# Local masks written into the score banks by ScalarE, for the next group, in place of TensorE's two identity products

## What is computed

```python
def local_attention(q, k, v):          # w = 32, 8 windows a sequence
    bk2, bv2 = (look(bk), look(bv))    # keys of the window before and of its own: 64
    mask = (it < jb) | (it > jb + w) | (jb == -1)
    sim = jnp.einsum('bhwie,bhwje->bhwij', bq, bk2) * QK_SCALE
    sim = jnp.where(mask, -jnp.finfo(sim.dtype).max, sim)
    attn = jax.nn.softmax(sim, -1)
    return jnp.einsum('bhwij,bhwje->bhwie', attn, bv2)

for i in range(DEPTH):                 # 6
    x = attn_layer(shift_tokens(x), Wqkv[i], q_scale[i], k_scale[i], Wo[i]) + x
    x = ffn_layer(shift_tokens(x), ln_g[i], ln_b[i], W1[i], b1[i], W2[i], b2[i]) + x
```

## Time and profile before

| | |
|---|---|
| median of 3 runs | 1949.55 us (1947.46 to 1950.31) |
| the profiled execution, its own time | 1953.01 us |
| its span | 1951.2 us |
| TensorE busy | 1860.3 us, 95% |
| VectorE busy | 1581.5 us, 81% |
| ScalarE busy | 1405.6 us, 72% |
| GpSimd busy | 1372.8 us, 70% |
| mask products L940 | 384, busy 73.6 us |
| granted TensorE clock, mean | 0.997 |

### The profile page before, as it was taken

The page is one execution under the profiler, slowest core; times in us unless marked ns, Lnnn a source line. Parts: engine busy times, 40 slices in busy tenths (PEclk is TensorE's granted clock), DMA queues, the critical chain, the costliest instruction groups (busy, mean ns, idle before and its releaser), DMA issues.

```text
span 1951.2 us, 68794 instructions
## 1 busy us (share of the span) xinstructions
PE 1860.3 (95%) x27097; PEld 1396.0 (72%) x27097; DVE 1581.5 (81%) x3053; ACT 1405.6 (72%) x2846; POOL 1372.8 (70%) x1458
## 2 busy tenths in 40 slices
PE   5999998999999999999999999999999999999998
PEld 4777765777777777777777677777777776777774
DVE  5776777888888888888888888888888878888875
ACT  3666665577777777777777777777777777777784
POOL 4010023888898787898788987878987879878780
PEclk9999999999999999999999999999999999999999
DMA  4000001344433345333434333343343343434332
GB/s 133 1 1 0 0 0 30 92 105 106 127 87 103 96 104 127 92 92 102 103 98 127 88 102 99 101 127 93 93 103 97 102 128 83 108 94 104 95 97 68
DMA packets 193542, 171.20 MB, mean 88 GB/s; under 512 B 32304, under 2 KB 190168, under 8 KB 193240
## 3 DMA queue, kind: packets, MB, share of 16 engines
q1 hardware_dynamic: 193240, 167.02, 32.8%
HBM read 21.14 MB, written 1.05 MB: 11 GB/s over the span
## 4 chain that ended last, share of the span: by engine, by line
PE 71%; ACT 12%; issue 7%; DVE 4%; POOL 3%; SPq 2%; DMA 0%; ACTq 0%; POOLq 0%; DVEq 0%
PE bank L971 7%; PE bank L933 7%; PE bank L901 6%; PE pair_bank L949 6%; PE bank L980 5%; PE bank L959 3%; PE bank L1032 3%; PE bank L981 3%; PE bank L982 3%; PE bank L1054 3%; ACT sq L616 2%; SPq L353 2%; PE bank L818 2%; PE bank L1046 2%; PE pair_bank L940 2%
## 5 line engine op out<-in xcount | busy, mean ns | idle before, releaser
L429 POOL TENSOR_TENSOR z_raw<-rot_u,rot_v 128x256 f32<-128x256 f32 x768 | 553.4, 745 | 102.8 <-DVE rot_v L1282 97.2
L422 POOL TENSOR_TENSOR z_norm<-probs_t,z_raw 128x512 f32<-128x512 f32 x376 | 482.0, 1282 | 92.7 <-DVE probs_t L1361 87.1
L1281 DVE TENSOR_TENSOR rot_u<-bank,tabs 128x512 f32<-128x512 f32 x384 | 263.1, 685 | 168.6 <-ACT sq L616 168.4
L449 POOL TENSOR_TENSOR sqs<-sq 128x512 f32<-128x512 f32 x192 | 245.7, 1280 | 89.5 <-issue 88.6
L980 PE MATMUL bank<-x_high,w_high 128*128 128x256 f32 x768 | 301.5, 393 | 0.2 <-issue 0.2
L681 ACT ACTIVATE pair_bank<-pair_bank 128x512 f32<-128x512 f32 x192 | 111.7, 582 | 220.8 <-DVE pair_bank L1262 220.6
L1282 DVE TENSOR_TENSOR rot_v<-bank,tabs 128x512 f32<-128x512 f32 x384 | 261.4, 681 | 0.0
L616 ACT ACTIVATE sq<-bank 128x512 f32<-128x512 f32 x384 | 225.2, 588 | 49.8 <-PE bank L982 43.6
L971 PEld LDWEIGHTS bank<-probs_t,v_late 128*64 128x64 f32 x3072 | 155.0, 137 | 144.4 <-issue 144.4
L625 ACT ACTIVATE probs_t<-bank 64x512 f32<-64x512 f32 x384 | 226.7, 590 | 35.6 <-PE bank L959 33.4
L933 PE MATMUL bank<-sqs,consts 128*128 128x512 f32 x384 | 199.0, 600 | 25.4 <-POOL sqs L449 25.4
(11 more groups left out here) (181 smaller groups left out, 4555.2 us busy)
## 6 DMA issues: line engine op xcount, KB each, us to landing
zqk<-z_norm SPq DMA_DIRECT2D x1536, 64.0 KB, 2.1
v_late<-v_sb SPq DMA_DIRECT2D x192, 192.0 KB, 2.6
w_qkv<-in_L_ffn_Wqkv SPq DMA_DIRECT2D x18, 512.0 KB, 4.9
v_late<-v_sb SPq DMA_DIRECT2D x192, 32.0 KB, 2.6
wo<-in_L_ffn_Wo SPq DMA_DIRECT2D x24, 128.0 KB, 2.3
w<-in_L_ffn_W SPq DMA_DIRECT2D x12, 170.5 KB, 3.4
z_norm<-in_L_attn_x SPq DMA_DIRECT2D x4, 256.0 KB, 5.4
w_qkv<-in_L_attn_w_kv_up SPq DMA_DIRECT2D x4, 256.0 KB, 5.1
```

Of the source, the lines that this page charges most:

```text
L422: return pool.tensor_tensor(z_norm[:, parity, idx, :, :], rinv(m)[:, idx, :].unsqueeze(1).broadcast_to([P, 2, T]), z_raw[:, parity, idx, : ...
L429: a = pool.tensor_tensor(z_raw[:, parity, idx, half, :], rot_u[:, idx, half, :], rot_v[:, idx, 1 - half, :], ALU.add)
L1281: dve.tensor_tensor(rot_u[:, idx, :, :], src, tabs[:, 2 * idx, :, :], ALU.mult)
```

## The change

TensorE makes the mask products for group 0 alone. For each later group, ScalarE copies the bf16 mask from SBUF into both score banks in one instruction (`lay_masks`), in the slot before: behind `output_out` and ahead of the gate copy, the GELU and the squares of q. It waits until VectorE has read the weights of the current group out of the banks. The scores wait for that copy (`mask_laid`) and no longer for `weights_ready` themselves.

```diff
--- before.py
+++ after.py
@@ -198,7 +198,7 @@
         names += """spread_zero w_in split_high split_done rot_par_ready q_tabs_ready k_tabs_ready gain_ready gate_bias_ready out_bias_ready
             x_high_ready x_split lk_done lq_done lv_done k_prod q_prod k_square q_square sums_ready k_summed q_summed
             n_done ln_done rinv_ready bound_ready zn_ready z_in0 z_in1 z_in2 z_in3 lv_ready v_late_in0 v_late_in1 v_late_in2 v_late_in3
-            scores_done top_ready shifted raised sum_ready part_ready weights_ready turned spread_ready lpv_done lyt_ready
+            scores_done mask_laid top_ready shifted raised sum_ready part_ready weights_ready turned spread_ready lpv_done lyt_ready
             wo_in0 wo_in1 wo_in2 wo_in3 lwo_done lres_done xc_done xc_ready xc_squared var_done ln_var rstd_ready xh_raw xh_ready
             w1_gate_in w1_up_in w2_in gate_done gate_ready gelu_done up_done hid_ready mlp_done mlp_res""".split()
         S = {n: sem(n) for n in names}
@@ -643,6 +643,11 @@
                 act.wait_ge(S["xc_ready"], w + 1)
                 after(act, "var_done", w)
                 act.activation(xc2[:, :], xc[:, :], ACT.Square).then_inc(S["xc_squared"], 1)
+
+            def lay_masks(n):
+
+                act.wait_ge(S["weights_ready"], n)
+                act.activation(pair_bank[:, :, 0:4 * KEYS], mask_b["local"][:, :].unsqueeze(1).broadcast_to([P, 2, 4 * KEYS]), ACT.Copy).then_inc(S["mask_laid"], 1)
 
             def output_out(n):
 
@@ -702,6 +707,8 @@
                     gained((s - 8) // G)
                 if four:
                     output_out(s - 1)
+                if active(s, 0, GROUPS - 1):
+                    lay_masks(s + 1)
                 for c in range(3):
                     if mlp_slot(s, 13 + c):
                         p = (s - 13 - c) // (2 * G)
@@ -935,9 +942,11 @@
             def windows(n, unit, g):
 
                 pe.wait_ge(S[f"z_in{g}"], 16 * 2 * HG * (unit + 1))
-                after(pe, "weights_ready", n)
+                if n:
+                    pe.wait_ge(S["mask_laid"], n)
                 for a in range(2):
-                    pe.matmul(bank[a][:, 0:4 * KEYS], ident_b[:, :], mask_b["local"][:, :], start=True, stop=True)
+                    if n == 0:
+                        pe.matmul(bank[a][:, 0:4 * KEYS], ident_b[:, :], mask_b["local"][:, :], start=True, stop=True)
                 for pair in range(2):
                     for x in range(2):
                         for tile in range(TILES):
```

## The result

| | predicted | measured |
|---|---|---|
| time after, median | 1931.2 us (1923 to 1943) | 1965.75 us (1963.77 to 1968.11, 4 runs) |
| time before, on the same chip | | 1949.93 us (1947.46 to 1952.33) |
| change | -18.4 us | +15.8 us; after/before 1.0083, 95% interval 1.0068 to 1.0098 |

The kernel became slower by 0.8%, where 0.85 had been put on faster. The profiled execution took 1968.11 us (span 1966.3), against 1953.01 us (span 1951.2) before: +15.1 us.

What follows compares the result with a forecast made beforehand. The prediction took TensorE to bound the kernel, with 71% of the chain of waits. Mask products gone -29.5, copies in the GELU stretch +10.6, first slots +0.5: -18.4 us, so 1931.2 us from 1949.55, range 1923 to 1943.

Steps and rivals of the forecast that it cites:

- Who waits for the squares of q: Slots from 1041 to 1070: ScalarE-VectorE ring with three copies 27.72 us, TensorE 27.76; a tie, TensorE leading by 0.04.
- Its new waits: Copy's waits on ScalarE and the scores' wait on TensorE: claimed to cost nothing, no wait put into the sum.
- The products' gain: Mask products leaving TensorE: 0.22 us a slot, 144 pairs on the chain, less 2.2 at layer changes: 29.5 us gained.
- The GELU stretch: Once in 8 slots, ScalarE without a gap from L685 to yt: one copy inside, 22 x 0.48 = 10.6 us lost.
- The copy's pitch: ScalarE's mask copy from start to start: taken as 0.48 us, read behind yt, with 0.69 as upper bound.
- (a): ScalarE's gapless 12.1 us around the GELU, once in 8 slots, on the chain 22 times; one copy falls inside.
- First slots: Start of the kernel, where SyncE's DMA queue sets the pace: one copy ahead of it costs 0.5 us.
- (b): Change of layers, five times: GpSimd sets the time, so mask products removed there give nothing, 2.2 us less gain.
- The 0.2 us between the copy and the scores: Tightest place found: copy ends at 1049.25, first score product comes at 1049.44, so TensorE's scores never wait.
- Rival 2: ScalarE becomes the bound with a copy at 0.80 us, slower from 0.74 on: +8.8, 1958.4 us; chance 0.07.
- Rival 1: The ScalarE-VectorE ring takes over with a copy at 0.60 us, 28.08 against 27.76: -8.8, 1940.8 us; chance 0.20.
- Theory A: Set up for the experiments: the loss is TensorE's wait at bank 3, from the gate copy's place in ScalarE's queue.

Runs made afterwards that it cites:

- e2: Against the changed kernel, neither mask copies nor TensorE's mask products for groups 1 to 191, so scores stay without a mask: 1924.3 us.
- e7: Against the changed kernel, copies behind the gate copy and none for slots 1 and 6 or the last four groups, where TensorE's products stay: 1929.4 us.
- e8: Against e7, slot 6 also gets its copy, behind the gate copy, and the next slot's gate copy is put ahead of yt: 1937.2 us.
- e1: Against the changed kernel, the mask copy stands behind the MLP gate's copy instead of ahead of it, all else the same: 1944.5 us.
- e5: Against the changed kernel, copies only for slots 2 to 5 past the first groups, each preceded by an unread copy into SBUF; TensorE's products elsewhere: 1949.5 us.
- e6: Against the kernel before, a single copy in eight slots, slot 6's, ahead of the gate copy, in groups 14 to 187 only: 1951.3 us.
- e9: Against e8, slot 6's copy stands ahead of its gate copy and all gate copies are behind yt: 1933.3 us.

## Why the prediction was wrong

**The step that failed** is "Who waits for the squares of q", and with it "Its new waits". The first followed the ring of ScalarE and VectorE from the squares of q only to L685, compared it there with TensorE, and found a tie. The second named the gate copy as one of the things "behind it" on ScalarE, and then asked only whether yt and the scores wait. Who waits for the gate copy was never asked. It is TensorE's L1068 and L1076, for bank 3. Followed to there, the ring is at 16.18 against 15.34 us in slot 6, and in slot 7 the distance of 0.83 us says that there is no margin. Slots 6 and 7: +19.0 us where the sum had about -8.

Point by point:

- *The products' gain*, 29.5 us: right in mechanism and near in size; e2 measures 27.0. Slot 2, whose mask products were on the chain, gives only 0.08, held by `hid` at bank 3: the same kind of wait as in slots 6 and 7, and as little looked for.
- *The GELU stretch*, 10.6 us: measured 10.4, for the right reason, though by 0.49 a slot and 21 periods; e7 and e8, which leave that copy out, have 0.00 there.
- *The copy's pitch*, 0.48: mis-sized. I read the distance behind the instruction in front of the copy, not behind the copy; it measured 0.52 to 0.62. By itself this is worth little here (one copy more dear in (a), three in the ring less its 0.04: 22 x (0.04 + 0.08) = 2.6 us).
- *First slots*, +0.5 us: not to be told. They gave -2.3 in the changed kernel and between -0.6 and -2.4 in most others, but the start of slot 1 scatters by as much, and at slot 17 the changed kernel was 0.1 us behind.
- *The change of layers*: slot 5 there is 0.25 longer even in e2, where there is no copy. Slots 3 and 4 there are 0.22 and 0.10 shorter, and in slot 5 TensorE's norms then wait for GpSimd, which they didn't before. So this is the prediction's (b): GpSimd, without a gap there, sets the time, and what was gained is given back. Of e2:

```profile
1100.75 1.10 PE L938 MATMUL bank<-sqs,consts 128*128 128x512 f32 x2 [0.37 <-POOL sqs L449]
```

- *The 0.2 us between the copy and the scores*: held in the change (0.3 us of waits in all), and failed in e1 and e8, where the gate copy's 0.57 is put ahead of it, and in slot 2 of e5. The distance was right (0.21 us measured), but 0.14 of it is what a held start needs (e1: 982.67 to 982.80), so the margin was 0.07, and I did not look where it would be used up.
- *Rival 2* came out on the measured side (1958.4 against 1965.75), but not by its mechanism: the copy took 0.60 us, not 0.74 or more. e1, with as many copies in another order, and e5's slots 3 to 5 show that ScalarE's load isn't the bound. Rival 1's sign for the ring was right and its end point, L685, was wrong too.
- *What would show it*: TensorE's share of the chain (53% for 70%) and slots 6 and 7 contradict the forecast; slots 3, 4, 5 and 0, the GELU stretch and the copy's length agree with it. No sign was set for a wait at the products for the layer norm, which is what came.

Theory A explains slots 6 and 7 of the change. For slot 7 it is shown by e1, where the order of two instructions alone takes its 0.51 us away. For slot 6 it rests on the recorded waits for the gate copy, on e6 and e9 with one copy in the ring (15.69 and 15.68 us, for 15.66 worked out) and on the change with two (16.20 for 16.18). The second mechanism, the scores' wait in slot 6, came to it through e1, e8 and e9. Not settled: the first and the last slots.

## What to carry to other kernels

When an instruction is put into an in-order queue, list every instruction behind it with its consumer on the bound engine, and measure for each how far the consumer's start lies behind the producer's end. Compare this with the distance at a place where the wait is recorded (0.14 us here, 0.82 to 0.84 from the gate copy's start); where it is no more, there is no margin, even if the idle time shown is zero. That the distance is the same in all periods isn't enough: slot 6 had 1.15 or 1.16 us in 22 of 23 and a margin of 0.33. A PSUM bank that two stages share is such a consumer, and it is found in the waits of the code, not in the name of the data. An operation that is free in some slots and dear in others needn't be moved everywhere: six slots of eight gave 1.1% where all eight gave -0.8%.

## What the runs showed of the hardware

- The copy of 512 values a partition from bf16 in SBUF into PSUM took 0.601 us and 0.52 to the next start; a bf16 tile into a bf16 tile in SBUF (e5) took 0.627 us. Instructions of 512 values that read PSUM gave way after 0.48 (yt, the squares).
- The start of TensorE's product lay 0.81 to 0.84 us behind the start of the ScalarE copy of 0.68 or 0.69 us that it waited for, so about 0.14 us from its end to TensorE's start; the same was seen behind the mask copy (982.67 to 982.80) and, at 0.14 or 0.15, behind VectorE's `hid` (e2).
- A pair of TensorE's products of 256 columns took 0.67 us where it was held by a wait and 0.59 where it wasn't, though the profile often records no idle time ahead of the held ones (slot 7 before, slot 2 in e2).
- Scores accumulated by TensorE onto values that ScalarE had written to PSUM; the changed kernel's masked attention is computed so. Within the stack only group 0 had a product of TensorE that starts the accumulation in those banks.
